# A selective-scan block: 15 of 64 weighings on GpSimd, the scan writing over its input

## What is computed

```
x = x + 0.5 * ffn(layernorm(x))
x = x + mamba(layernorm(x))
x = x + 0.5 * ffn(layernorm(x))

ffn(x):   xr, xk = mix of x and x one token earlier, by mu_r and mu_k
          sigmoid(xr @ W_r.T) * (square(relu(xk @ W_k.T)) @ W_v.T)

mamba(x): xs, z = split(layernorm(x) @ W_in.T)             # 1024 channels each
          xc = silu(causal convolution of xs, 4 taps)
          dt_low, B, C = split(xc @ W_xproj.T)             # 32, 16, 16
          delta = softplus(dt_low @ W_dt.T + b_dt)
          h[t] = exp(delta[t] * A) * h[t-1] + delta[t] * B[t] * xc[t]   # 16 states a channel
          y[t] = sum over the states of h[t] * C[t]
          out = ((y + D_skip * xc) * silu(z)) @ W_out.T + residual
```

## Time and profile before

| | us |
|---|---|
| median of 3 runs | 4893.23 (4893.09 to 4894.3) |
| span of the profiled execution | 4888.0 |
| busy in it: TensorE | 4296.9 (88%) |
| busy: VectorE | 4488.3 (92%) |
| busy: ScalarE | 2900.1 (59%) |
| busy: GpSimd | 3196.4 (65%) |
| mean granted clock of TensorE | 0.971 |
| first scan starts | 153.6 |
| last scan starts | 4779.8 |

### The profile page before, as it was taken

One profiled execution on the slowest core, in us unless ns is written; L12 is line 12 of the kernel. 1 busy time (PEld: TensorE's weight loads), 2 busy tenths in 40 slices (PEclk: granted clock), 3 DMA queues, 4 the chain that ended last, 5 costly groups with the idle time before them and its releaser, 6 DMA issues.

```text
span 4888.0 us, 58099 instructions
## 1 busy us (share of the span) xinstructions
PE 4296.9 (88%) x16896; PEld 2382.9 (49%) x16896; DVE 4488.3 (92%) x3650; ACT 2900.1 (59%) x6355; POOL 3196.4 (65%) x3328
## 2 busy tenths in 40 slices
PE   6777989898999989989898899989999898999787
PEld 2444545454554545545454454545545454554443
DVE  2799999999999999999999999999999999999992
ACT  2555656666666566656666665666656666665452
POOL 1666767576676767767576676767667576776770
PEclk9888999999999999999999999999999999999798
DMA  2445555454554555555555554555555565655451
GB/s 82 141 135 180 172 171 185 163 183 162 189 169 151 189 168 186 172 173 185 158 174 163 186 172 152 190 179 176 172 185 173 155 180 156 190 170 153 167 164 62
DMA packets 423053, 810.71 MB, mean 166 GB/s; under 512 B 41264, under 2 KB 41264, under 8 KB 418640
## 3 DMA queue, kind: packets, MB, share of 16 engines
q1 hardware_dynamic: 422736, 807.00, 52.1%
HBM read 772.25 MB, written 34.60 MB: 165 GB/s over the span
## 4 chain that ended last, share of the span: by engine, by line
DVE 38%; PE 29%; issue 16%; ACT 7%; POOL 6%; DMA 3%; DVEq 0%; SPq 0%; POOLq 0%; ACTq 0%
DVE decay L1091 19%; DVE g L1099 10%; PE y_acc L567 6%; PE mm L494 5%; PE mm L483 5%; POOL dbx L1298 4%; PE mm L472 4%; DVE xc L1037 3%; DMA c_all<-bc_scratch 2%; PE mm L531 2%; PE mm L509 2%; PE mm L519 2%; DVE xc L1043 1%; ACT decay L889 1%; POOL xout L1287 1%
## 5 line engine op out<-in xcount | busy, mean ns | idle before, releaser
L1298 POOL TENSOR_TENSOR dbx<-u,b_all 128x1024 f32<-128x1024 f32 x1024 | 2414.2, 2358 | 902.6 <-DVE g L1099 901.7
L1091 DVE TENSOR_TENSOR_SCAN decay<-decay,state,dbx 128x1024 f32<-128x1024 f32 x1024 | 2405.4, 2349 | 172.4 <-ACT decay L889 157.6
L567 PE MATMUL y_acc<-ident,g 128*128 128x128 f32 x8192 | 1124.2, 283 | 372.5 <-DVE g L1099 370.6
L567 PEld LDWEIGHTS y_acc<-ident,g 128*128 128x128 f32 x8192 | 947.4, 144 | 939.1 <-DVE g L1099 713.2
L1099 DVE TENSOR_TENSOR g<-decay,c_all 128x1024 f32<-128x1024 f32 x1024 | 1244.3, 1215 | 10.0 <-DMA c_all<-bc_scratch 1.1
L886 ACT ACTIVATE decay<-delta,neg_a 128x512 f32<-128x512 f32 x1024 | 708.7, 692 | 36.9
L889 ACT ACTIVATE decay<-delta,neg_a 128x511 f32<-128x511 f32 x1024 | 686.9, 671 | 0.0
L895 ACT ACTIVATE state<-decay 128x2 f32<-128x2 f32 x1024 | 166.9, 163 | 508.6 <-DVE g L1099 506.1
L494 PE MATMUL mm<-wbuf_c,col 128*128 128x512 f32 x1024 | 460.9, 594 | 2.1 <-ACT col L758 1.3
L1037 DVE SCALAR_TENSOR_TENSOR xc<-mm,conv_sb,xc 128x509 f32<-128x509 f32 (+2 forms) x384 | 285.3, 743 | 47.0 <-ACT xs_last L804 35.7
L1302 POOL TENSOR_TENSOR dbx<-dbx,carry 128x1 f32<-128x1 f32 x1024 | 274.2, 268 | 80.3
(11 more groups left out here) (100 smaller groups left out, 5107.4 us busy)
## 6 DMA issues: line engine op xcount, KB each, us to landing
b_all<-bc_scratch SPq DMA_DIRECT2D x1024, 256.0 KB, 3.4
c_all<-bc_scratch SPq DMA_DIRECT2D x1024, 256.0 KB, 3.6
wbuf_d<-in_w_r SPq DMA_DIRECT2D x32, 1024.0 KB, 7.5
wbuf_c<-in_w_v SPq DMA_DIRECT2D x32, 1024.0 KB, 7.3
xin<-in_x SPq DMA_DIRECT2D x16, 1024.0 KB, 6.8
wbuf_c<-in_w_k SPq DMA_DIRECT2D x16, 1024.0 KB, 6.7
wbuf_d<-in_w_in SPq DMA_DIRECT2D x16, 1024.0 KB, 5.8
wbuf_a<-in_w_in SPq DMA_DIRECT2D x16, 1024.0 KB, 8.0
```

The source lines that it names most:

```text
L567: last = pe.matmul(y_acc[:, tb, j * P:(j + 1) * P], g[:, s % PAIRS, j, tb * P:(tb + 1) * P], ident[:, :], start=n == 0 and j == 0 and tb % ...
L1091: dve.tensor_tensor_scan(d, d, flat(dbx[:, s % DBX, :, :]), state[:, batch, s, 0:1], ALU.mult, ALU.add).then_inc(scan_done, 1)
L1298: pool.tensor_tensor(dbx[:, s % DBX, :, :], u[:, q % 2, :, :], b_all[:, s % BRING, :].unsqueeze(1).broadcast_to([P, QT, W]), ALU.mult).the ...
```

## The change

- `POOL_WEIGH` names 15 steps (1, 5, 9, ..., 57). In these the scan writes h to `dbx` in SBUF, over its own input, and not to `decay`. VectorE doesn't weigh them: GpSimd does, `g = dbx * c_all` (`pool_weigh`), behind the product of the step that `POOL_WEIGH_AT` names, two or three steps later. Its semaphore is `pool_weighed`; `weighed(it, s)` tells those who wait for step s which of the two semaphores to wait for. `save` reads h from `dbx` in these steps and waits for the scan alone. The product that takes this buffer of `dbx` next waits for `pool_weighed` and `saved`.
- The one-column add of `carry` goes from GpSimd to ScalarE, ahead of the step's decays. It waits for the product; so the decays of a step now wait for its product too.
- `ZEROS` is empty.
- The tables place other work anew, most of it by one or two steps; `BANK` and `LOAD` change with them.

The core of the diff (of the tables, those lines that the text below speaks of):

```diff
+        pool_weighed = sem("pool_weighed")
-        MM_K = ((5, 7, 8, 9), (46, 47, 50, 51))
+        MM_K = ((5, 6, 8, 9), (46, 48, 50, 52))
-        XPROJ = (49, 50)
-        ZEROS = {2: 2, 31: 2, 39: 2, 30: 1, 53: 1}
+        XPROJ = (47, 49)
+        POOL_WEIGH = (1, 5, 9, 13, 17, 21, 25, 29, 33, 37, 41, 45, 49, 53, 57)
+        POOL_WEIGH_AT = (3, 7, 12, 15, 19, 24, 27, 31, 36, 39, 43, 47, 51, 55, 59)
+        ZEROS = {}
-        MIX_K = ((3, 4, 5, 5), (42, 43, 45, 46))
-        MIX_R = ((6, 7, 7, 8), (38, 39, 40, 40))
-        CSILU = (33, 34, 40, 42, 43, 45, 48, 48)
+        MIX_K = ((3, 4, 5, 5), (42, 43, 45, 45))
+        MIX_R = ((6, 7, 7, 9), (36, 38, 40, 40))
+        CSILU = (33, 34, 43, 43, 44, 46, 49, 49)
...
+        def weighed(it, s):
+
+            n = NSTEP * it + s
+            if n < 0:
+                return None
+            it, s = divmod(n, NSTEP)
+            if s in POOL_WEIGH:
+                return pool_weighed, ON_POOL[NSTEP] * it + ON_POOL[s] + 1
+            return mult_done, (NSTEP - ON_POOL[NSTEP]) * it + s - ON_POOL[s] + 1
...
             def sum_g(it, s):
-                pe.wait_ge(mult_done, NSTEP * it + s + 1)
+                pe.wait_ge(*weighed(it, s))
...
             def make_decay(it, s):
+                act.wait_ge(dbx_done, NSTEP * it + s + 1)
+                first = dbx[:, s % DBX, 1, 0:1]
+                act.activation(first, first, ACT.Identity, bias=carry[:, q % 2, n:n + 1]).then_inc(decay_done, 1)
...
             def scan(it, s, batch):
-                d = flat(decay[:, s % PAIRS, :, :])
-                dve.tensor_tensor_scan(d, d, flat(dbx[:, s % DBX, :, :]), state[:, batch, s, 0:1],
+                d, v = flat(decay[:, s % PAIRS, :, :]), flat(dbx[:, s % DBX, :, :])
+                dve.tensor_tensor_scan(v if s in POOL_WEIGH else d, d, v, state[:, batch, s, 0:1],
                                        ALU.mult, ALU.add).then_inc(scan_done, 1)
...
             def product(it, s):
+                if (s - DBX) % NSTEP in POOL_WEIGH:
+                    pool.wait_ge(saved, NSTEP * it + s - DBX + 1)
+                    pool.sem_inc(passed_pool, 1)
...
-                pool.wait_ge(dbx_done, 2 * (NSTEP * it + s) + 1)
-                pool.tensor_tensor(dbx[:, s % DBX, 1, 0:1], dbx[:, s % DBX, 1, 0:1], carry[:, q % 2, n:n + 1],
-                                   ALU.add).then_inc(dbx_done, 1)
+
+            def pool_weigh(it, s):
+                pool.wait_ge(scan_done, NSTEP * it + s + 1)
+                pool.wait_ge(c_loaded[s % CRING], it * (16 * NSTEP // CRING) + 16 * (s // CRING + 1))
+                pool.sem_inc(passed_pool, 1)
+                if due(count := NSTEP * it + s - PAIRS + 1):
+                    pool.wait_ge(g_summed, count)
+                pool.tensor_tensor(g[:, s % PAIRS, :, :], dbx[:, s % DBX, :, :],
+                                   c_all[:, s % CRING, :].unsqueeze(1).broadcast_to([P, QT, W]),
+                                   ALU.mult).then_inc(pool_weighed, 1)
```

105 lines of the change are left out of this document (57 added, 48 removed), and 6 rows, old and new, of the table BANK.

## The result

The changed kernel takes 5020.4 us (median of 4 runs, 5015.4 to 5023.6), the kernel before 4893.4 beside it: ratio 1.0261, 95% interval [1.0246, 1.0275]. It is slower by 127 us, where 4800 was predicted.

A forecast was written before the change was run, and what follows sets the result against it. No engine bounds it throughout: VectorE limits steps 25 to 44, TensorE 4 to 24 and 45 to 60. Middle iterations gain 5 us each (70), first and last 10 and 14: 94 off 4888.0, said as 4800; range 4700 to 4905.

The forecast's parts named there:

- Zero products: Taking them out saves TensorE 0.9 us per iteration in steps 45 to 60, and nothing elsewhere.
- By stretch: Weighing on GpSimd counts fully only where VectorE is last: 11.7 of 18.2 us per middle iteration, before anything is added.
- the port: VectorE's mixes and silus, reading two SBUF operands, wait for GpSimd's multiplies: about 9 us added VectorE time per iteration.
- GpSimd's chain "just fits": Multiply, product, carry add and decays take some 6.8 us against VectorE's 7.1 until scan s+3; costed at nothing.
- The scan into SBUF: On 15 steps per iteration the scan writes SBUF and keeps 2.35 us; bounds 0.1 less to 2.36 more.
- The add on ScalarE: 64 carry adds of about 0.16 us, 10 us per iteration, bring ScalarE to 191 of 280 us; it fits.
- The mixes: 24 mixes and silus per middle iteration wait longer, at steps 3, 5, 34, 43, 45, 49; mean 1.1 to 1.3 us.
- The law of 0.55 us plus the rest of the multiply: A VectorE mix starting during a GpSimd multiply takes 0.55 us plus what is left of that multiply.
- The sum's ends: First and last iteration, where VectorE is last, gain 10 and 14 us; head and tail hold no step.
- The clock: TensorE's clock stays above 0.96; as a rival (0.1), at 0.95 all 5 us are gone, 4893 within 10.
- The port takes all and more: Rival (0.15): longer mixes eat the gain; at 0.75 us on each of the 24, 100 us slower, 4990.
- GpSimd's chain goes the same way: Within the port rival (0.15): the chain of 6.8 against 7.1 us also slows once mixes hold up GpSimd's products.

The follow-up runs named there:

- front half: The kernel before with the new places and banks only for the work of steps 0 to 24 and the gates and transposes moved from 66 to 67: 4965.7 us.
- back half: The kernel before with the new places and banks only for the work of steps 25 to 63: 4955.3 us.
- loads: The kernel before with only the new steps of SyncE's loads and stores and ScalarE's copies of the residual: 4902.0 us.
- one-input mixes: 384 mixes and silus replaced by a one-input statistics instruction: changed kernel 4869.1 us, with all weighing on VectorE 4960.6, kernel before 4829.7.
- the square: The changed kernel with 15 or no steps weighed on GpSimd, each with two-input or one-input mixes: 5020, 5053, 4869 and 4961 us.

## Why the prediction was wrong

The sum went from 4888 to 4794. On the chip the same way has two legs: places, zero products and carry add +160 (forecast at about nothing), and weighing -33 (forecast -94). The first leg is 160 of the 221 us by which 4800 missed 5020. This split holds for the places first, which is how the prediction worked (it walked the new order). With the weighing first the legs are +300 (weighing and add at the old places, 5192) and -171 (the new places, to 5020). In either order what failed is the same: the sum has no price for the order of the work, neither for what the moved work holds up nor for what GpSimd's late results do.

**The tables had no term.** The prediction went through weighing, GpSimd's chain, the add and the mixes, and for all the other work that changed its place it had a sentence for the zero products and part of one for x_proj. This is the step that failed. In the kernel before: front half +73, back half +63, loads +8, zeros +31. For the one move of the front half that was followed, what it takes to see it was in the trace of before: which bank the matmuls for the step sizes wait for, and what stands ahead of the instruction that empties it.

**Zero products: wrong.** They were given a gain of 0.9 us per iteration in steps 45 to 60. Taking all out of the kernel before cost 31 us; in a stretch where TensorE is idle for half a microsecond, taking one out gained nothing. The earlier trace rows gives a product's time; without it half of that came back as idle time of TensorE, and the clock fell later.

**By stretch: the way was right, the size was not.** Before the port, 11.7 of 18.2 us per iteration were to count. Without the port weighing gained 91 us, 5.3 per middle iteration (295.7 to 290.4, mean of 12, between the two kernels with one-input mixes). Steps 0 to 3 gave 0.9 (forecast 1.2), 4 to 24, where TensorE is last, 1.4 (1.5), and 25 to 44 4.2 (6.1); four steps there gave nothing (29 to 32). The term that failed is steps 45 to 60: 2.9 forecast, 0.9 of it for zero products that neither of these two kernels has, so 2.0 for weighing; measured -0.3, with 53 to 56 slower by 0.9. And 61 to 63 got slower by 0.9.

**GpSimd's chain "just fits": wrong.** It was checked against the scans and called free, with 0.3 us of cover. The scan waits for its decays 291 us in all against 158 in the earlier trace rows, and 199 in the changed kernel with all weighing on VectorE. Not followed at all was who else waits for GpSimd: TensorE's sum, and behind it in TensorE's order the transposes and matmuls (2.73 us at the one place shown, 365.2 us of waits in all at the old places).

**The scan into SBUF: right,** 2342 ns, at the value taken and inside the bounds of the earlier trace rows. The one of step 5 writes SBUF beside GpSimd's product and both keep their time; 98 of the 240 run beside a product or multiply of GpSimd, 2344 ns in the mean, the others 2340. By the rule of the Trainium skill in "SBUF — State Buffer", Who interferes with whom, a VectorE instruction with at most one SBUF input, outside the 2-port performance modes, does not contend with GpSimd; these scans agree.

**The add on ScalarE: mis-sized, harmless.** 0.16 us were estimated, 288 ns measured. It costs 11 us in the kernel before and is worth 52 in the changed one, where it relieves GpSimd. The prediction counted it as load taken off GpSimd, but not as time gained.

**The mixes: right.** About 9 us per iteration were forecast, 10.0 measured in a middle iteration (20.9 us of mixes and silus before, 30.9 after). By place: step 3 +0.8 (forecast 0.9), step 5 +1.9 (2.1), step 45 +1.9 (2.1), step 49 +1.9 against the same silus at 48 (2.1). Step 34 had nothing (1.4), and step 43 +1.0 (0.5) against the kernel whose VectorE weighs everything. Missed were step 6 with +2.0 and step 9 with +1.7. Of all 384 the mean is 1.26 us (forecast 1.1 to 1.3). The law of 0.55 us plus the rest of the multiply held: in the changed kernel 185 mixes and silus start while GpSimd has over 0.2 us left of a product or multiply, and every one of them takes what is left plus 0.546 to 0.555 us. Weighing made the mixes 8.4 us longer per middle iteration (22.5 to 30.9), some 128 us in all, of which the square puts 58 us on the path.

**The sum's ends.** First and last iteration were to gain 10 and 14 us; they came to +10.9 (slower) and -7.4. A middle iteration was to take 286 to 287 us and steps 25 to 44 about 95; the means are 300.1 and 101.3. The head was said to hold no step; its first scan is 7.5 us later.

**The clock.** "Above 0.96" was wrong: 0.954. It isn't what loses most: with the zero products back it is 0.965 and the kernel is 11 us slower, and the two halves of the places lose 136 us at 0.97. Which part of the 127 us the lower clock holds wasn't isolated.

**The rivals.** "The port takes all and more" came near with its 4990, but by luck: in the new places weighing still gains 33 us with all its waits at the port. The port is a part all the same: with one-input mixes the loss is 39 and not 127 us. "GpSimd's chain goes the same way" was the better half of it. No rival said that the moved work itself costs; beside two-input mixes that is 160 us, and 131 beside one-input ones.

What stays open: in the front half only one move is priced alone (20 of 73 us), in the back half one group of moves (-34, in a half that loses 63). Which of the others costs what wasn't tried. Nor was a search for places that suit GpSimd's weighing; that no such places gain isn't shown.

## What to carry to other kernels

When a change moves work that another part of it doesn't force, price the moved places as an edit of their own, and first: for each moved instruction follow the buffer or bank that it empties to the next engine that waits for it. When work goes to a slower engine, list all that wait for its result and what stands behind them in order; the free time of the slower engine says little. And look for the single stall in the timeline before: moving x_proj and what stands beside it by one or two steps gained 34 us, as much as 240 multiplies moved to another engine.

## What the runs showed of the hardware

- A one-column add with a bias from a tile takes 288 ns on ScalarE (a one-column copy of zeros 160), against 268 on GpSimd.
- Two two-input instructions of VectorE in a row beside a multiply of GpSimd: 3.49 us for both, and the multiply 2.65 in place of 2.36. The engine whose instruction starts second waits, on either side; a mix or silu of VectorE that starts second takes 0.55 us plus what is left of GpSimd's instruction (185 of them in the changed kernel).
- Removing a multiply of 1.215 us between two scans shortens a step by 1.27 us: successive scans overlap by 0.09.
- Zero products raise the granted clock (0.954 to 0.965 in the changed kernel) and still cost 11 us there, while in the kernel before they are worth 31 us (0.952 to 0.971).
